# Experts over sorted blocks: tokens scattered to their two experts' regions and gathered back by index

## What is computed

```python
def moe_ff(x, gate_w, w1, w2, w3):
    xf = x.reshape(b * t, d)
    scores = xf @ gate_w
    topk_scores, topk_idx = jax.lax.top_k(scores, TOPK)          # TOPK = 2 of 8 experts
    topk_probs = jax.nn.softmax(topk_scores, axis=-1)
    weight = jnp.sum(jax.nn.one_hot(topk_idx, EXPERTS) * topk_probs[..., None], axis=1)
    h = jax.nn.silu(jnp.einsum('td,edh->eth', xf, w1)) * jnp.einsum('td,edh->eth', xf, w2)
    out_e = jnp.einsum('eth,ehd->etd', h, w3)                    # d = 128, h = 256
    out = jnp.einsum('etd,te->td', out_e, weight)
    return out.reshape(b, t, d)
...
h = layernorm(x, ln2_scale, ln2_shift)
x = x + moe_ff(h, gate_w, w1, w2, w3)
```

## Time and profile before

| | us |
|---|---|
| median of 3 runs | 2064.76 (2063.63 to 2065.24) |
| profiled execution, its own time | 2060.17 |
| its span | 2058.6 |
| TensorE busy | 1542.1 (75%) |
| VectorE busy | 1280.6 (62%) |
| ScalarE busy | 1040.3 (51%) |
| GpSimd busy | 345.7 (17%) |
| mean granted TensorE clock | 0.886 |

### The profile page before, as it was taken

How to read it: one execution, slowest core, us unless ns; L and a number is a source line. 1 busy time by engine, 2 the same in 40 slices (tenths; PEclk the granted TensorE clock), 3 DMA queues, 4 the chain that set the end, 5 groups by cost and what they waited for, 6 DMA issues and landing times. The chain is left out here.

```text
span 2058.6 us, 49422 instructions
## 1 busy us (share of the span) xinstructions
PE 1542.1 (75%) x19079; PEld 972.4 (47%) x19079; DVE 1280.6 (62%) x3055; ACT 1040.3 (51%) x1996; POOL 345.7 (17%) x677
## 2 busy tenths in 40 slices
PE   6534277777539999995525888898899897888747
PEld 3212144444326666662213555555566555555423
DVE  6943677777156676663313677676777676777636
ACT  4433066667333322323424677676777675776333
POOL 4433145555240000002200000000000000000023
PEclk8867599999769999997767999999999999999869
DMA  2148222222352122114879999999999999999522
GB/s 72 42 136 269 57 54 67 67 66 48 97 173 85 57 83 87 57 62 136 266 182 361 351 381 375 383 377 378 392 379 380 370 337 371 366 378 373 153 63 62
DMA packets 132551, 431.76 MB, mean 210 GB/s; under 512 B 37296, under 2 KB 85328, under 8 KB 114736
## 3 DMA queue, kind: packets, MB, share of 16 engines
q1 hardware_dynamic: 108512, 248.86, 36.0%
q10 hardware_dynamic: 13104, 150.80, 18.4%
q0 software_dynamic: 10720, 29.11, 5.5%
HBM read 225.41 MB, written 203.03 MB: 208 GB/s over the span
## 5 line engine op out<-in xcount | busy, mean ns | idle before, releaser
L2138 DVE CUSTOM_DVE_ANT_0 r_shifted<-r_ps_ac,r_shifted 128x512 f32<-128x512 f32 x512 | 351.9, 687 | 270.3 <-PE r_ps_ac L2013 228.4
L2104 ACT ACTIVATE r_probs<-r_ps_keys 128x512 f32<-128x512 f32 x512 | 309.8, 605 | 218.8 <-PE r_ps_keys L2020 195.4
L2083 ACT ACTIVATE r_wide<-r_ps_wide 128x512 f32<-128x512 f32 (+1 forms) x576 | 329.9, 591 | 92.0 <-PE r_ps_wide L2004 91.6
L2020 PE MATMUL r_ps_keys<-r_ident,r_shifted 128*128 128x128 f32 x2048 | 323.6, 282 | 15.9 <-issue 9.3
L2020 PEld LDWEIGHTS r_ps_keys<-r_ident,r_shifted 128*128 128x128 f32 x2048 | 265.3, 146 | 63.4 <-issue 22.5
L2004 PE MATMUL r_ps_wide<-r_r,r_qv 128*32 128x96 bf16 (+12 forms) x6144 | 235.6, 254 | 66.1 <-issue 51.2
L2146 DVE TENSOR_SCALAR r_shifted<-r_shifted,r_mx 128x512 f32<-128x512 f32 x512 | 249.2, 487 | 18.3
L912 ACT ACTIVATE c_probs<-c_ps_keys 128x512 f32<-128x512 f32 (+1 forms) x384 | 174.2, 531 | 141.6 <-PE c_ps_keys L838 141.5
L2013 PE MATMUL r_ps_ac<-r_k,r_qu 128*128 128x512 bf16 x512 | 206.6, 404 | 27.2 <-DMA r_k<-stack 22.4
L2004 PEld LDWEIGHTS r_ps_wide<-r_r,r_qv 128*32 128x32 bf16 x6144 | 104.0, 97 | 166.3 <-issue 165.6
L1474 ACT ACTIVATE e_silu<-e_ps_a 128x1024 f32<-128x1024 f32 x64 | 65.7, 1027 | 216.1 <-PE e_ps_a L1407 216.0
(11 more groups left out here) (216 smaller groups left out, 2104.1 us busy)
## 6 DMA issues: line engine op xcount, KB each, us to landing
skew<-r_wide ACTq DMA_DIRECT2D x64, 2224.0 KB, 13.8
r_shifted<-skew SPq DMA_DIRECT2D x64, 2160.0 KB, 14.9
e_weight_all<-weights SPq DMA_DIRECT2D x8, 2048.0 KB, 7.7
c_qk<-qk_stacks POOLq DMA_DIRECT2D x64, 192.0 KB, 3.8
stack<-d_part SPq DMA_DIRECT2D x96, 128.0 KB, 2.6
qk_stacks<-b_part SPq DMA_DIRECT2D x48, 128.0 KB, 3.5
qk_stacks<-b_part POOLq DMA_DIRECT2D x48, 128.0 KB, 3.7
stack<-d_part POOLq DMA_DIRECT2D x48, 128.0 KB, 3.6
```

The lines of the kernel that those rows point to most:

```text
L2020: last = pe.transpose(ps_keys[u % 2][:, j * P:(j + 1) * P], shifted[:, s, W * u + j * P:W * u + (j + 1) * P], ident[:, :])
L2083: act.activation(wide[:, s, c, lo:hi], ps_wide[bk % BANKS][:, 0:hi - lo], ACT.Copy).then_inc(wide_sb, 1)
L2104: act.activation(probs[:, h % 2, :, b * P:(b + 1) * P], ps_keys[u % 2][:, :].rearrange("p (j i) -> p j i", j=NT), ACT.Exp, scale=SCALE).th ...
L2138: dve.tensor_tensor_reduce(out=shifted[:, s, W * u:W * u + L], in0=ps_ac[u % 2][:, :], in1=shifted[:, s, W * u:W * u + L], scale=1.0, scal ...
```

## The change

Each token is now computed by its two experts only.

In DRAM there is a table `by_expert` of SORTED = 34816 rows of 128 features: a region of 4096 rows for each expert and 2048 rows behind. `phase_attention` fills it with zeros: POOL sets a `blank` of 128 x 8704 elements first of all, and ACT issues four DMAs of 4.4 MB after the first image's exponentials.

`phase_route` takes the place of `phase_merge` at that point and does the routing too. Beside the merge's work TensorE transposes z, makes the scores, and ranks each choice in its expert's list by products with a lower triangle and with ones. VectorE finds the two best, marks them (`hot`), keeps a running count (`run`) and computes each choice's row (`pos`). POOL scatters: for each image 8 indirect DMAs of 128 rows of 512 bytes. VectorE at the end makes `table`: for each of BLOCKS = 39 blocks its expert and its first row in `by_expert`. `base`, the probabilities `pr`, `hot` and the places stay in SBUF; nothing but the scattered rows is stored.

`phase_blocks` takes the place of the experts' work. 39 is the most blocks of 256 rows that 8192 choices can need, and all 39 always run. For each block SP reads its row and its expert from the table into a register, and loads the block's 256 rows and that expert's w1, w2 and w3, 128 KB each, into one of four slots. TensorE transposes, ACT scales, shifts and applies silu, VectorE multiplies, TensorE multiplies by w3, with no float32r halves; VectorE takes the sums and ACT stores them to `expert_out`.

`phase_combine` takes the place of `phase_project` for d_ and of the experts' last steps. POOL gathers each image's rows of its two choices (8 indirect DMAs of 128 rows), VectorE multiplies them by the probabilities, adds `base` and normalizes, SP stores x2. Then come the projections as before, with the term stores by SP (12) and ACT (6).

```diff
+REGION = NB * L
+BT = 256
+BLOCKS = (2 * REGION - NE) // BT + NE
+SORTED = NE * REGION + NE * BT
...
 phase_attention
+            pool.memset(blank[:, :], 0.0).then_inc(blank_set, 1)
             norm.constants(pool)
...
             take_operands(1)
+            act.wait_ge(blank_set, 1)
+            for i in range(FILLS):
+                act.dma_start(zeros_out.rearrange("(i p r) d -> i p (r d)", i=FILLS, p=P)[i], blank[:, :])\
+                    .then_inc(filled, 16)
...
 phase_route (sync)
+                if n == 2:
+                    sp.dma_start(gate[:, :], gate_in).then_inc(route_loaded, 16)
...
 phase_route (gpsimd)
+            def scatter(n):
+                pool.wait_ge(pos_ready, n + 1)
+                for r in range(2):
+                    for t in range(NT):
+                        k = NT * r + t
+                        pool.indirect_dma_start(sorted_out[:, :], bass.IndirectOffsetOnAxis(pos[:, n, k:k + 1], 0),
+                                                z[:, n, t, :], None).then_inc(scattered, 16)
...
 phase_route (tensor)
+            for n in range(NB):
+                project(n)
+                if n + 2 < NB:
+                    invert(n + 2)
+                if n >= 2:
+                    rank(n - 2)
+                if n >= 1:
+                    score(n - 1)
+                turn(n)
...
 phase_route (vector)
+            for n in range(NB):
+                if n + 1 < NB:
+                    divide(n + 1)
+                merge(n)
+                if n >= 2:
+                    place(n - 2)
+                if n >= 1:
+                    take_scores(n - 1)
+                    best(n - 1)
+                    mark(n - 1)
...
 phase_blocks (sync)
+            def load_tokens(b):
+                row = sp.value_load(table[0:1, 1, b:b + 1], min_val=0, max_val=SORTED - BT)
+                if b >= SLOTS:
+                    sp.wait_ge(x_ps, b - SLOTS + 1)
+                sp.dma_start(x[:, b % SLOTS, :, :],
+                             sorted_in[bass.DynSlice(row, BT), :].rearrange("(t p) d -> p t d", p=P))\
+                    .then_inc(x_loaded[b % SLOTS], 16)
+
+            def load_weights(b):
+                s = b % SLOTS
+                e = sp.value_load(table[0:1, 0, b:b + 1], min_val=0, max_val=NE - 1)
+                if b >= SLOTS:
+                    sp.wait_ge(y_ps, b - SLOTS + 1)
...
+            for b in range(BLOCKS):
+                load_tokens(b)
+                load_weights(b)
...
 phase_combine (gpsimd)
+            gather(0)
+            norm.constants(pool)
...
+            pool.memset(v9[:, :, :, :], 1.0).then_inc(ones_set, 1)
+            gather(1)
+            for n in range(NB):
+                norm.root(pool, n + 1)
+                if n + 2 < NB:
+                    gather(n + 2)
```

More of the change, by code:

```diff
@@ new lines, in _, with take_tokens, activate, store @@
+        @block.scalar
+        def _(act):
+            def take_tokens(b):
+                act.wait_ge(x_ps, b + 1)
+                if b >= 2:
+                    act.wait_ge(b_ps, b - 1)
+                act.activation(hT[:, b % 2, :], ps_x[b % 2][:, 0:BT], ACT.Identity, bias=sc[:, 1:2], scale=sc[:, 0:1])\
+                    .then_inc(hT_sb, 1)
+            def activate(b):
+                act.wait_ge(a_ps, b + 1)
+                if b >= 2:
+                    act.wait_ge(gu_sb, b - 1)
+                act.activation(silu[:, b % 2, :, :].rearrange("p k t -> p (k t)"), ps_a[b % 2][:, :], ACT.Silu)\
+                    .then_inc(silu_sb, 1)
+            def store(b):
+                act.wait_ge(y_sb, b + 1)
+                act.dma_start(y_out[BT * b:BT * (b + 1), :].rearrange("(t p) d -> p t d", p=P),
+                              y[:, b % SLOTS, :, :]).then_inc(stored[b % SLOTS], 16)
+            take_tokens(0)
+            for b in range(BLOCKS):
+                if b + 1 < BLOCKS:
+                    take_tokens(b + 1)
+                activate(b)
+                if b >= 2:
+                    store(b - 2)
+            store(BLOCKS - 2)
+            store(BLOCKS - 1)
@@ L1355, in _ @@
         @block.gpsimd
         def _(pool):
-            def low_tokens(n, s):
-                pool.wait_ge(hT_high, n + 1)
-                pool.tensor_tensor(hT_halves[1][:, s, :], hT[:, s, :], hT_halves[0][:, s, :],
-                                   ALU.subtract).then_inc(hT_low, 1)
-            def step(it, s, first, ahead):
-                n = 2 * it + s
-                for e in range(NE):
-                    if e == 0 and ahead:
-                        low_tokens(n + 1, 1 - s)
-                    if e == 3 and not first:
-                        norm.root(pool, n)
@@ L1370, in _, with gather @@
[L1370 to L1373 removed]
+            def gather(n):
+                if n >= YS:
+                    pool.wait_ge(second_added, n - YS + 1)
+                for r in range(2):
+                    for t in range(NT):
+                        k = NT * r + t
+                        pool.indirect_dma_start(y[:, n % YS, r, t, :], None, y_in[:, :],
+                                                bass.IndirectOffsetOnAxis(pos[:, n, k:k + 1], 0))\
+                            .then_inc(gathered[n % YS], 16)
@@ L1375, in _ @@
+            gather(0)
+            norm.constants(pool)
+            for c in range(NC):
+                if biases[c] is None:
+                    pool.memset(bias[:, c:c + 1], 0.0).then_inc(ones_set, 1)
+            pool.memset(v9[:, :, :, :], 1.0).then_inc(ones_set, 1)
+            gather(1)
+            for n in range(NB):
+                norm.root(pool, n + 1)
+                if n + 2 < NB:
+                    gather(n + 2)
         @block.tensor
         def _(pe):
-            HALVES = ((0, 0), (0, 1), (1, 0))
@@ L1387, in route @@
+            pe.wait_ge(consts, n_const)
+            turn(0)
+            for n in range(NB):
+                pe.wait_ge(xT_sb, n + 1)
+                for c in range(NC):
+                    if n >= 1:
+                        pe.wait_ge(rest1_ready, NC * (n - 1) + c + 1)
+                    pe.matmul(ps_c[c][:, :], w[:, c, :], xT[:, n % 2, :], start=True, stop=True).then_inc(c_ps, 1)
+                if n >= 1:
+                    pe.wait_ge(v_sb, n)
                 for t in range(NT):
-                    last = pe.matmul(ps_s[:, t * NE:(t + 1) * NE], hT[:, s, t * P:(t + 1) * P], gate[:, :],
+                    last = pe.matmul(ps_v[:, t * P:(t + 1) * P], xT[:, n % 2, t * P:(t + 1) * P], w[:, NC, :],
```

959 lines of the change are left out of this document (645 added, 314 removed).

## The result

The changed kernel takes 1985.66 us (median, 1965.66 to 1999.26), the kernel before beside it 2065.0 (2063.63 to 2067.0): a ratio of 0.9605, 95% interval 0.9565 to 0.9645. (The ratio is of fast runs alone; the slowest of the four after, 1999.26 us, counts as slow and stands in the median but not in the ratio.) The forecast was 1980. The profiled execution of after has a span of 1963.9 us against 2058.6, 94.7 less, at the low end of its runs.

A forecast was written before the change was run, and what follows sets the result against it. No engine bounds the merge, TensorE the experts, DMA the projections. +75.1 for merge with routing, -192.4 for blocks and +32.4 for projections give -84.9 us: 1975 from the profiled execution, 1980 as forecast median, range 1920 to 2060.

The forecast's parts named there:

- Fill and attention: Attention: writing 17.8 MB of zeros takes some 57 us and ends near 80, before the stage does at 122; cost 0.
- The scatters' start: Merge with routing: POOL's scatters begin at 584.2 us, after three rounds and the ranking of image 0.
- two rounds of 3.9: Merge with routing: after the first round at 563.95 + 3, two more POOL rounds of 3.9 us each.
- 6 us more until VectorE has ranked image 0: Merge with routing: a wait of 6 us after those rounds, before the third round of 3.4 and the scatters.
- C: POOL's cost of one indirect DMA of 128 rows: 1.1 us, between bounds of 0.53 and 2.1; 64 in the merge.
- rival that they are dear: Indirect DMAs cost more than forecast: gain gone at 1.95 us each, kernel 2086 us at 2.1; chance 0.08.
- SP as the pace: Blocks: SP's four DMA issues, register work and two reads take 3.73 us a block; stage 152.5 us against 344.9.
- TensorE's own 2.95: Blocks: TensorE's transposes and plain f32 matmuls take 2.95 us a block, 115 us for 39, under SP's 3.73.
- rival of a sinking clock: Blocks: TensorE's clock drops, a block takes 5.2 us and the stage 57 longer, 2037 us in all; chance 0.08.
- rival in which they land late: Blocks: weight loads need 8 us to land, making 4.35 us a block and 2004 us in all; chance 0.12.
- That covers POOL (8 C + 1.3 = 10.1): Combine: the DMA time of 14.8 us an image hides POOL's eight gathers and root, 10.1 us an image.
- 14.8 us an image: Combine: DMA bounds the projections at the old rate, 26.5 MB in 118.4 us after the first transpose; stage 140.4 us.

The follow-up runs named there:

- run 4: The changed kernel with TensorE's transposes of z moved behind the next image's projection: merge 137.4 us instead of 141.3, total 1972.62 us, ratio 0.9597.
- run 3: The changed kernel without its 64 scatters, all routing arithmetic kept, output not the layer's: merge 101.2 us instead of 141.3, total 1938.45 us.
- run 5: The changed kernel with the blocks' weight loads and the expert read moved from SP to POOL: blocks 121.5 us instead of 141.1, total 1953.73 us, ratio 0.9511.
- run 6: The changed kernel with two more register reads by SP in each block: blocks 181.1 us instead of 141.1, total 2009.36 us.
- run 7: The changed kernel with the second image's gathers behind POOL's first root: combine 137.8 us instead of 134.7, total 1980.45 us, ratio 0.9609.
- run 9: The changed kernel with 32 of its 64 gathers, output not the layer's: combine 111.2 us instead of 134.7, total 1964.22 us.

## Why the prediction was right, and where it wasn't

**Fill and attention: right.** The stage ends at 120.8 us instead of 120.5, with the DMA share at 0.52. The fill was quicker than forecast: with it the DMA engines are full from 20 to 60 us, at 414 to 449 GB/s where 310 was taken, and from 70 us on the share is 0.14 again. The memset took 7.35 us (8.0 forecast) under its cover.

**Merge with routing: 17.6 us too short.** Four terms (the rounds between the scatters are the missing 0.2):

- The scatters' start. Forecast 36.3 us into the stage (584.2 - 547.9), measured 40.4. Failed step: "two rounds of 3.9". They took 9.0 each, 10.3 us more together, since the order of TensorE's queue chains a round to the transposes of the one before (run 4). The "6 us more until VectorE has ranked image 0" fell away in return, since the ranks were there by then: from the third round to the first scatter 3.5 us passed. +4.1 in all.
- C. Forecast 1.1, measured 1.27 from start to start, 0.96 in the instruction and 0.30 behind it. The bounds, 0.53 and 2.1, held it. +10.6 for 64, and the rival that they are dear (over 1.95) is refuted. The working "twice the plain one" had no gap between two instructions in it, and that is the 0.30.
- Landing: forecast 3.5, measured 1.3 (679.87 to 681.2). -2.2.
- The drain. Forecast nothing beside 0.4 of barrier, measured 5.29; run 3 shows whose it is. +5.3. This is the one term that was missing and not mis-sized.

The rounds and biases between the scatters were 13.1 in the forecast and are 12.9 (93.9 from the first start to the last end, less 81.0). POOL as the pace of the stage from the first scatter on was right; that its start hangs on an order in TensorE's queue was not seen.

**Blocks: 11.4 us too long.** SP as the pace: right (runs 5 and 6). The size of its block: 3.73 in the forecast, 3.36 measured. The issues were taken at 0.47 and are 0.34 to 0.38 plus 0.1 between two. For a read 0.8 was taken and 0.25 of register work a block beside: 1.85 for two reads, where the two gaps are 1.52. The Trainium skill ("DMA: Bandwidth & Descriptors", Latency and other measured facts) gives a `tensor_load` a floor of about 600 ns; for a read from SBUF on SP this case shows less, 0.273 us in the instruction and, in a row of such reads, 0.51 each (run 6). A stage worked out with that floor, an estimate from the page, would have been 136.9 us, nearer to the 141.1 measured than the 152.5 of the forecast. Ahead of the first load of tokens 1.4 us passed (0.5 forecast), and behind the last one 12.2 (10.2, its block included). TensorE's own 2.95 was confirmed by run 5, 2.84. The granted clock was 1.00 from 700 to 800: the rival of a sinking clock is refuted. TensorE waits 10% of the stage and not the 20% foretold (9.9 us of 100, all for e_x), as SP's block is shorter. Loads land in 2.3 to 2.4 us (medians), under the 8 of the rival in which they land late.

**Combine: 5.7 us too long, and by the wrong engine.** The first transpose came at 24.8 (852.75 - 827.96) against 22.0, nearly all of it from C. But the failed step is "That covers POOL (8 C + 1.3 = 10.1)". Behind the transpose 109.9 us passed, and not the 118.4 that the DMA rate of before gave. This is POOL between two roots in the middle of the stage:

```profile
887.62 1.04 POOL L123 TENSOR_TENSOR d_norm_rstd<-d_norm_var_eps,d_norm_consts 128x4 f32<-128x4 f32 x1
888.85 1.00 POOL L1917 DMA_INDIRECT d_y<-expert_out,x_pos  x1 [0.19 <-issue]
890.15 2.40 POOL L1917 DMA_INDIRECT d_y<-expert_out,x_pos  x1 [0.30 <-issue]
...
900.40 1.03 POOL L123 TENSOR_TENSOR d_norm_rstd<-d_norm_var_eps,d_norm_consts 128x4 f32<-128x4 f32 x1
```

12.8 us an image (900.40 - 887.62) without a wait for a semaphore: 1.4 for the root, eight gathers at 1.25, and 1.4 more for the one that takes 2.40. That long one is not spread at random. VectorE's row beside it:

```profile
889.82 1.89 DVE L2043 TENSOR_TENSOR d_part<-d_rest,d_part 128x512 bf16<-128x512 f32 x3
```

The gather starts at 890.15, during these three subtractions, and ends at 892.55, 0.8 us behind them. So it is with every gather over 2 us in after and in runs 7 and 9 (the subtractions are L2044 in run 7); in run 9 it is the fourth behind the root and not the second, and again it is the one beside L2043. VectorE's work thus lengthens POOL's chain by some 1.4 us an image. That one holds the other is what the rows suggest; no run moves the subtractions to show it.

DMA needs less than the 14.8 us an image of the forecast. These 14.8 were the 101.9 us of before, with the end of the stage in them, over eight images. At the 269 GB/s of the earlier trace rows the 3.3 MB of an image are 12.3 us, an estimate from these numbers, and already under POOL's 12.8; and DMA can do 310 in this stage (run 9). A share of 0.89 was read as "bound by DMA". In after a share of 0.88 was not the bound; whether it was in the stage of before, no run tests. By the forecast's own rule (wrong "if the projections are paced by another than DMA") this part was wrong, and only its size close: 109.9 for 118.4.

**Sum.** +17.6, -11.4 and -5.7 leave 0.5. The forecast of 1980 lay within 6 us of the median for a reason that no step of it may claim: two overpriced guesses paid for a drain and a queue order that were not in it and for a C that was too cheap. That is luck. The range of 1920 to 2060 held, and each unknown stayed within its bounds; that is what the bounds were for.

## What to carry to other kernels

When a stage gets a new kind of instruction, price its gap and the end of the stage as well as its duration: a drain of 4 to 5 us stood in the trace of before at every stage whose DMAs POOL issued. It is paid where POOL is the last to finish and free where another engine is. A queue that issues transfers from registers is an engine to be costed like any other, and moving part of it to an idle queue was worth more here (19.6 us) than any other edit that keeps the result. Call a stage bound by DMA only if its share is as high as the same trace shows elsewhere (0.88 at 272 GB/s is not, where another stage shows 1.00 at 371), and look at the stages rather than the median where one stage varies by 20 us by itself.

## What the chip showed that was not expected

- POOL's drain at the end of a stage in which it issued DMAs: 5.29 us with all of them landed, 0.06 without them; 6.35 behind 64 gathers and 3.74 behind 32.
- An indirect DMA of 128 rows of 512 bytes holds POOL for 0.96 us and 0.30 more pass before the next; the data are there 1.3 us after the last. One gather in eight took 2.2 to 2.4 us instead of 0.95 in the middle of the combine stage, always the one beside VectorE's three subtractions of L2043; the cause was not tested.
- The stage of relative positions, with the same instructions at a full DMA, took from 878 to 898 us.
